# Self entries of the count banks written by ScalarE from a stored pattern in place of a product on TensorE

## What is computed

```
x = x + gnn(layernorm(x), stack([src, dst]))
x = x + ffn(layernorm(x))

gnn:  h = relu(x @ W1 + b1) @ W2 + b2
      return h + segment_sum(h[dst], src)          # row = src, col = dst
ffn:  weights = normalised max(softmax(x @ Wg + bg) - 0.25 * sigmoid(x @ Wt + bt), 0)
      return sum over 8 experts of weights[:, e] * (x @ We[e] + be[e])
```

## Time and profile before

| | before |
|---|---|
| median of 3 runs | 387.11 us (387.05 to 387.25) |
| the profiled execution | 388.22 us, span 386.4 us |
| PE busy | 368.4 us, 95% |
| DVE busy | 286.3 us, 74% |
| ACT busy | 105.1 us, 27% |
| POOL busy | 6.1 us, 2% |
| L904 counting products | 402 records, mean 270 ns |
| L896 self products | 50, mean 273 ns |
| L429 evictions | 50, mean 379 ns |
| L397 positions | 50, mean 715 ns |

### The profile page before, as it was taken

How to read it: one execution, slowest core, us unless ns; L and a number is a source line. 1 busy time by engine, 2 the same in 40 slices (tenths; PEclk the granted TensorE clock), 3 DMA queues, 4 the chain that set the end, 5 groups by cost and what they waited for, 6 DMA issues and landing times.

```text
span 386.4 us, 5935 instructions
## 1 busy us (share of the span) xinstructions
PE 368.4 (95%) x1892; PEld 240.3 (62%) x1892; DVE 286.3 (74%) x440; ACT 105.1 (27%) x189; POOL 6.1 (2%) x33
## 2 busy tenths in 40 slices
PE   0999999999989999999989999999999999999996
PEld 0877787666656563567656666666666666666663
DVE  3799986999989939882798765757658557666653
ACT  4734355555676303545110010010010100100000
POOL 6000000000000000000000000000000000000000
PEclk9999999999999998999999999999999999999999
DMA  8970011222222205310020200200301100000223
GB/s 178 246 241 16 15 40 32 80 67 77 76 73 84 85 23 131 133 59 2 1 77 34 75 36 1 109 0 0 109 0 59 50 0 0 0 0 0 76 86 105
DMA packets 16808, 23.87 MB, mean 62 GB/s; under 512 B 2796, under 2 KB 9683, under 8 KB 16660
## 3 DMA queue, kind: packets, MB, share of 16 engines
q1 hardware_dynamic: 16382, 23.05, 20.2%
q10 hardware_dynamic: 403, 0.53, 0.6%
HBM read 14.77 MB, written 2.56 MB: 45 GB/s over the span
## 4 chain that ended last, share of the span: by engine, by line
PE 81%; DVE 11%; issue 3%; DVEq 3%; DMA 1%; ACT 0%; ACTq 0%
PE ps_g L986 17%; PE ps_g L987 17%; PE ps_g L988 17%; PE ps_g L866 10%; PE ps_w L904 8%; DVE split L635 4%; PE ps_g L942 4%; PE ps_g L852 2%; DVE stats L600 2%; DMA dst_i<-in_dst_dram 1%; DVE x_sb L762 1%; PE ps_w L896 1%; DVE x_sb L767 1%; PE ps_w L942 1%; DVEq L651 1%
## 5 line engine op out<-in xcount | busy, mean ns | idle before, releaser
L986 PE MATMUL ps_g<-we_hi,split 128*125 128x512 f16 x304 | 115.4, 380 | 1.0 <-DVE x_sb L762 1.0
L988 PE MATMUL ps_g<-we_hi,split 128*125 128x512 f16 x304 | 115.2, 379 | 0.0
L987 PE MATMUL ps_g<-we_lo,split 128*125 128x512 f16 x304 | 115.2, 379 | 0.0
L635 DVE TENSOR_TENSOR split<-places,keys 125x1536 f16<-125x1536 int16 (+2 forms) x125 | 91.1, 793 | 7.0 <-PE ps_w L904 4.3
L762 DVE SCALAR_TENSOR_TENSOR x_sb<-ps_g,weight_s,x_sb 125x512 f32<-125x512 f32 x76 | 56.9, 749 | 52.1 <-PE ps_g L988 52.1
L767 DVE SCALAR_TENSOR_TENSOR x_sb<-late,weight,x_sb 125x512 f32<-125x512 f32 x80 | 59.9, 750 | 9.5 <-DVE x_sb L762 5.3
L986 PEld LDWEIGHTS ps_g<-we_hi,split 128*125 128x125 f16 x304 | 41.5, 137 | 25.2 <-DVE x_sb L762 1.4
L988 PEld LDWEIGHTS ps_g<-we_hi,split 128*125 128x125 f16 x304 | 41.5, 137 | 24.1
L987 PEld LDWEIGHTS ps_g<-we_lo,split 128*125 128x125 f16 x304 | 41.5, 137 | 23.7
L904 PE MATMUL ps_w<-split 125*128 125x250 f16 x402 | 53.5, 270 | 2.3 <-DVE split L635 1.3
L866 PE MATMUL ps_g<-late,r_sb 125*128 125x512 f32 (+3 forms) x120 | 50.6, 530 | 0.0
(11 more groups left out here) (143 smaller groups left out, 220.5 us busy)
## 6 DMA issues: line engine op xcount, KB each, us to landing
stage<-in_L_ffn_W_exp_dram SPq DMA_DIRECT2D x8, 1024.0 KB, 5.4
late<-counts SPq DMA_DIRECT2D x50, 122.1 KB
x_sb<-in_x_dram SPq DMA_DIRECT2D x5, 448.0 KB, 10.9
out_dram<-x_sb SPq DMA_DIRECT2D x10, 224.0 KB
late<-in_L_ffn_b_exp_dram SPq DMA_DIRECT2D x1, 2000.0 KB
w_sb<-in_L_gnn_W_dram SPq DMA_DIRECT2D x2, 512.0 KB, 11.2
x_sb<-in_x_dram ACTq DMA_DIRECT2D x1, 260.0 KB
out_dram<-x_sb ACTq DMA_DIRECT2D x10, 26.0 KB
```

The costliest lines, as they stand in the source:

```text
L635: nc.vector.tensor_tensor(hot[hot_at(w, p)][:, 0:n, :].rearrange("p c (k x j) -> p (c k) x j", k=SEGS, j=2), places[w % WPT][:, 0:n, :].re ...
L986: nc.tensor.matmul(bank, xhi[:, k, tokens[i]], hi_w, start=(k == 0), stop=False)
L987: nc.tensor.matmul(bank, xhi[:, k, tokens[i]], lo_w, start=False, stop=False)
L988: mm = nc.tensor.matmul(bank, xlo[:, k, tokens[i]], hi_w, start=False, stop=(k == KD - 1))
```

## The change

The self entries are no longer multiplied on TensorE. GpSimd stores the whole pattern for all windows in one tensor, `self_rows` (128 partitions, 5 x 475 columns, float16): a memset and one `affine_select`. For each window ScalarE copies a slice of 250 columns of it into the bank (`fill_bank`), and the counting products add to that. Both banks are opened once, with two products of zeros (`start=True`); every later product in them has `start=False`. The fill of window w + 2 stands in `block_out(w)`, behind the eviction and a wait of ScalarE for that eviction (`win_out`), ahead of the positions. TensorE waits for the fill (`bank_filled`) where it waited for the eviction; the read of the step count stands right behind that wait. At the start, ScalarE waits for the pattern and for the opened banks, and fills both, between low positions 2 and positions 2; TensorE opens the banks behind the second turned tile, ahead of the sums over columns (L839).

```diff
--- before.py
+++ after.py
@@ -92,8 +92,7 @@
 
 
         ident = sb("ident", [128, 128])
-        self_pos = sb("self_pos", [128, SEG + HI - 1], F16)
-        self_lo = sb("self_lo", [128, 2 * LO - WIN], F16)
+        self_rows = sb("self_rows", [SEG, HI, 2 * LO - WIN], F16)
 
 
         iota_pos = sb("iota_pos", [EP, PART, SEG], I16)
@@ -207,6 +206,7 @@
 
         const_base, const_ready = sem("const_base"), sem("const_ready")
         lo_ready, self_base, self_ready = sem("lo_ready"), sem("self_base"), sem("self_ready")
+        bank_open, bank_filled = sem("bank_open"), sem("bank_filled")
         keys_placed = sem("keys_placed")
         prep, keys_ready = sem("prep"), sem("keys_ready")
         keys_turned, hits_ready, hits_turned = sem("keys_turned"), sem("hits_ready"), sem("hits_turned")
@@ -372,14 +372,12 @@
                                             base=-FIXED[m - 1][0], pattern=[[0, 1]], channel_multiplier=1).then_inc(first_ready, 1)
 
             nc.gpsimd.memset(zeros[:, :], 0.0).then_inc(self_ready, 1)
-            nc.gpsimd.memset(self_pos[:, :], 0.0).then_inc(self_base, 1)
-            nc.gpsimd.memset(self_lo[:, :], 0.0).then_inc(self_base, 1)
-            pool.wait_ge(self_base, 2)
-
-            nc.gpsimd.affine_select(out=self_pos[0:WIN, :], in_=self_pos[0:WIN, :], compare_op=ALU.not_equal, fill=1.0,
-                                    base=-(HI - 1), pattern=[[1, SEG + HI - 1]], channel_multiplier=-HI).then_inc(self_ready, 1)
-            nc.gpsimd.affine_select(out=self_lo[0:WIN, :], in_=self_lo[0:WIN, :], compare_op=ALU.not_equal, fill=1.0,
-                                    base=-(LO - WIN), pattern=[[1, 2 * LO - WIN]], channel_multiplier=-1).then_inc(self_ready, 1)
+            nc.gpsimd.memset(self_rows[:, :, :], 0.0).then_inc(self_base, 1)
+            pool.wait_ge(self_base, 1)
+
+            nc.gpsimd.affine_select(out=self_rows[:, :, :], in_=self_rows[:, :, :], compare_op=ALU.not_equal, fill=1.0,
+                                    base=HI * (LO - WIN), pattern=[[-1, HI], [-HI, 2 * LO - WIN]],
+                                    channel_multiplier=1).then_inc(self_ready, 1)
 
         @block.scalar
         def _(act):
@@ -420,6 +418,12 @@
                 act.wait_ge(ln1_rstd, i // 2 + 1)
                 nc.scalar.activation(r_sb[:, i, :], r_bank[i % 2], ACT.Relu, scale=rstd1[:, i:i + 1]).then_inc(r_ready, 1)
 
+            def fill_bank(w):
+
+                own_lo = LO - WIN - WIN * (w % (2 * WPT))
+                nc.scalar.activation(ps_w[w % 2][:, 0:LO], self_rows[:, w // (2 * WPT), own_lo:own_lo + LO],
+                                     ACT.Copy).then_inc(bank_filled, 1)
+
             def block_out(w):
                 q = w % WPT
                 if w >= WPT:
@@ -427,6 +431,9 @@
                     act.wait_ge(win_moved[q], 16 * (w // WPT))
                 act.wait_ge(win_done, w + 1)
                 nc.scalar.activation(counts[q][:, :], ps_w[w % 2][:, 0:LO], ACT.Copy).then_inc(win_out, 1)
+                if w + 2 < NW:
+                    act.wait_ge(win_out, w + 1)
+                    fill_bank(w + 2)
                 if w + WPT < NW:
                     positions(w + WPT)
 
@@ -443,6 +450,10 @@
                                  ACT.Copy).then_inc(keys_placed, 1)
             turned(0)
             low_places(2)
+            act.wait_ge(self_ready, 2)
+            act.wait_ge(bank_open, 1)
+            fill_bank(0)
+            fill_bank(1)
             positions(2)
             turned(1)
             low_places(3)
@@ -834,12 +845,17 @@
             for p in range(4):
                 pe.sem_inc(hot_used[p], 1)
             turn_x(1)
+            pe.wait_ge(keys_placed, 2)
+            pe.wait_ge(self_ready, 1)
+            for b in range(2):
+                opened = nc.tensor.matmul(ps_w[b][:, 0:LO], zeros[0:1, 0:128], zeros[0:1, 0:LO], start=True, stop=False,
+                                          skip_group_check=True)
+            opened.then_inc(bank_open, 1)
             pe.wait_ge(w1_in, 16)
             for k in range(KD):
                 mean = nc.tensor.matmul(mean_bank, ones[:, :], w1_sb[:, k, :], start=(k == 0), stop=(k == KD - 1))
             mean.then_inc(w1_mean, 1)
             pe.wait_ge(wtab_ready, 2)
-            pe.wait_ge(keys_placed, 2)
 
             def hidden(i):
                 if i == 0:
@@ -888,13 +904,7 @@
 
             def count(w):
                 bank = ps_w[w % 2]
-                i = w // WPT
-                own_lo = LO - WIN - WIN * (w % (2 * WPT))
-                if w >= 2:
-                    pe.wait_ge(win_out, w - 1)
-
-                nc.tensor.matmul(bank[:, 0:LO], self_pos[:, HI - 1 - i // 2:HI - 1 - i // 2 + SEG], self_lo[:, own_lo:own_lo + LO],
-                                 start=True, stop=False, skip_group_check=True)
+                pe.wait_ge(bank_filled, w + 1)
 
                 def one_step():
                     turn = pe.snap(turn_reg)
@@ -912,7 +922,6 @@
                 with pe.Fori(0, pe.value_load(wtab[0:1, NW + w:NW + w + 1])):
                     one_step()
 
-            pe.wait_ge(self_ready, 3)
             for w in range(NW):
                 count(w)
                 if w < WPT + LAG:
```

## The result

| | before | changed |
|---|---|---|
| median | 387.2 us (387.05 to 388.44, 5 executions) | 393.29 us (391.66 to 394.52, 5 executions) |
| ratio | | 1.0133, 95% interval 1.0108 to 1.0158 |
| span of the profiled execution | 386.4 us, mean granted clock 0.995 | 389.9 us, 0.999 |

The change costs 5.1 us by the ratio, 6.1 us by the medians. The page of the changed kernel: part 1, and the chain by engine and by line. They answer to the earlier trace rows.

A forecast was written before the change was run, and what follows sets the result against it. TensorE (95% busy) was taken as the bound; 5.4 us of products removed against a longer hand-over. Terms -0.5, -0.1, +0.3, +0.8, +0.5, +0.3 gave +1.3: median 388.4 us from 387.11, range 386.4 to 391.3.

The forecast's parts named there:

- the hand-over: Between windows sharing a bank: lengthened by the change, to 1.41 us from eviction start to first counting product.
- the release: On TensorE, from the fill's end to the first counting product, including the step count read: taken as 0.60 us.
- rival 1: At the start: GpSimd's long select holds VectorE's two-operand product 2.1 us; +3.4 in all, 390.5 us; chance 0.33.
- own eviction seen: On ScalarE, between eviction and fill: it must see its own eviction end, 0.03 us.
- fill 0.40: ScalarE's copy of 250 columns into the PSUM bank, taken as 0.40 us.
- ScalarE's round: ScalarE's work per window: grows from 0.88 to 1.33 us with the fill, in windows of some 1.5 us.
- rival 3: In the windows: fill 0.42, release 0.80 to 0.84 everywhere, ScalarE's lateness carried between groups; +3.5, 390.6 us; chance 0.08.
- The group with the cast: Windows 30 to 34: fills ahead of and behind ScalarE's 1.90 us cast add 0.45 each, about 0.1 in hand; +0.8.
- Windows 3 to 8: Early windows where TensorE sets the pace: windows 3 to 7 lose a product each, -0.5 us.
- Windows 9 to 17: Part of windows 8 to 17, where VectorE's run is the bound: at most -0.1 us more.
- The other edits: Later positions, opening products, first fills and GpSimd's longer writes: covered by slack, nothing added by themselves.
- Rival 2: In the windows: fill 0.30, release 0.50, hand-over short enough; -0.6 to -1.2, 386.5 to 385.9 us; chance 0.19.

The follow-up runs named there:

- late_select: The changed kernel with GpSimd's select waiting until VectorE has finished the step table's columns; median 391.73 us.
- no_fill: The changed kernel without fills and select, self entries left out, TensorE waiting for the eviction as before; ratio 0.9957 to the kernel before.
- the extra copy: The changed kernel with the same 250-column copy made once more, into SBUF, ahead of each fill; first compare to last eviction 126.6 us.

## Why the prediction was wrong

**The direction was right, and the hand-over as the cause in the windows; the size was not**, and the range (386.4 to 391.3) ended 2 us short of 393.29. Two steps failed: the hold of VectorE was left out of the sum, at nothing, where it cost 1.8 us; and the release in the hand-over was taken as 0.60 us, where it was up to 1.04 and the windows took 2.8 us more in place of 1.3. The clock, which stood nowhere in the prediction, added up to 1.4.

1. *The choice between the forecast and rival 1.* I gave the held VectorE 0.33 and put it beside the forecast, not into it, since no row of before had an overlap. It came as described: `hit` at 8.21 took 2.37 us in place of 0.36, 2.0 us more, where 2.1 was worked out (10.4 less 8.38 is 2.0). It started 0.17 earlier than before, as `dst` had landed earlier, which leaves +1.83 at the first compare. The overlap could be read off the rows: the select at 8.2 to 10.4, `hit` at 8.38. That no row of before showed one was no evidence against it, as the select of before was done by 7.53. Even with this term the sum would have been 390.5.

2. *The term that was mis-sized: the release.* I took 0.60 us, "because the waits that this makes leave the array idle". In most they don't: the fill ends while the cut of the window before still runs. From window 35 on, the third window of a group had a release of 0.58 to 0.76 us, the fourth 0.63 to 0.93 and the fifth 0.92 to 1.04. From the start of the eviction to the first product that made 1.37 to 1.56, 1.43 to 1.72 and 1.72 to 1.84 us, for the 1.41 forecast: it held in the third and was furthest out in the fifth. That the read behind the wait is the long part is shown by the run with the read first (0.22 us, windows 3.8 us shorter). Why it takes longer while the array still works is not shown. The other terms held: own eviction seen after 0.03 us (0.03), fill 0.40 (0.38), ScalarE's round 1.33 (fill to fill across an eviction at its tightest, 110.09 to 111.41, 1.32). With the 0.80 of rival 3 the same working gives +3.5 against +2.8 measured; a group grew by 0.5 us, not 0.15. In size rival 3 was nearer the truth for the windows than the forecast, and the earlier trace rows had shown a release of 0.84.

3. *The group with the cast.* Forecast +0.8 for windows 30 to 34; measured +1.06 (8.70 to 9.76 us). The excess is of the size of that of the other groups; what it comes of was not tested. The cast was no new cost: before, this group already took 0.9 us more than the two behind it (8.70, 7.76 and 7.80).

4. *Windows 3 to 8.* Forecast -0.5, measured -0.68 at window 8: right. Windows 9 to 17 likewise (-0.51 at window 18 against -0.6).

5. *The other edits.* The fills at the start cost nothing, as said: 0.04 us of difference in the first compare between `late_select` (15.69) and `no_fill` (15.65). The cover was there, to that extent.

6. *The clock.* Not in the sum at all. The changed kernel had a fall in 6 of 8 executions, the kernel before in 28 of 69. So the median of the changed kernel is that of an execution with a fall, and that of the kernel before (387.2, where full clock gives 385.0 to 385.4 of span) is not. That is the 1.4 us between the 4.7 of like executions and the 6.1 of the medians. With so few executions, that the change makes falls more frequent is not shown.

Sum: 1.8 (select) + 2.8 (windows, 1.06 of it in the group with the cast) is 4.6, for 4.7 in like executions; the other 1.4 of the 6.1 between the medians goes with the clock.

**Rival 2** needed a release of 0.50: it was not there, but 0.22 us is to be had by one line moved, and then the windows do become 1.0 us shorter than before. Its other ground, that PSUM is quicker to write, holds by 0.05 us.

## What to carry to other kernels

Before moving work off the busiest engine, write down the hand-over that the work stood in, from release to first useful instruction, with every sequencer step that the new order puts behind the wait; a register read that can stand ahead of a wait should. Then ask what the cheap preparation elsewhere runs beside: a one-off select of 2.2 us on an otherwise idle GpSimd cost as much as all the self products were worth. Price an edit by a kernel in which it is free: here that was 1.7 us of 5.4. And when a run gives the number that you expected, look where in the trace it comes from: the extra copy hit 126.5 with a fall of the clock in it.

## What the runs showed of the hardware

- A GpSimd select (reads and writes SBUF) and a VectorE product of two SBUF operands hold each other up: 2.37 to 2.40 us for 0.36 when the select is under way, and 2.40 for 2.21 us for the select when the product started 0.03 us ahead of it. A GpSimd memset leaves such a product alone (0.36 us); a `tensor_scalar` beside it took 1.09 for 0.41.
- A GpSimd memset of 2375 float16 columns takes 2.07 us, a select 2.21, on all 128 partitions.
- ScalarE writes 250 columns from SBUF (float16) into PSUM (float32) in 0.38 us, as long as it takes to read them out. Beside each other in one trace the same copy took 0.41 us into SBUF and 0.36 into PSUM.
- From the end of the fill that TensorE waits for to the first product: 0.22 us when the loop count is in a register, 0.58 us when it must be read and the array is idle, up to 1.04 us when it must be read and the array is still at work.
- Behind 1.9 to 2.3 us of idle time at the same place the granted clock fell from the 2.4 to the 1.2 GHz level for 3.4 us in three profiled executions, and stayed up in four.
